# Router of a mixture-of-experts layer in three stages with the mean square taken on rows, and a one-hot product on another engine

## What is computed

```
h      = hidden_states                                  # 4096 tokens x 128
hf     = h * rsqrt(mean(h * h) + 1e-6) * rms_weight
logits = hf @ gate_w.T                                  # 8 experts
e      = exp(logits - max(logits))
top 2 of e, divided by their sum                        # weights and experts
out    = sum over the two of weight * (silu(hf @ w1.T) * (hf @ w3.T)) @ w2.T
```

## Time and profile before

| | us |
|---|---|
| median of 3 runs | 1366.04 |
| lowest, highest | 1364.01, 1376.72 |
| profiled execution, its own time | 1369.83 |
| profiled execution, its span | 1368.0 |
| router, slots and the hand-overs between, 966.96 to 1083.1 | 116.1 |

### The profile page before, as it was taken

One profiled execution on the slowest core, in us unless ns is written; L12 is line 12 of the kernel. 1 busy time (PEld: TensorE's weight loads), 2 busy tenths in 40 slices (PEclk: granted clock), 3 DMA queues, 4 the chain that ended last, 5 costly groups with the idle time before them and its releaser, 6 DMA issues. The chain is left out here.

```text
span 1368.0 us, 23917 instructions
## 1 busy us (share of the span) xinstructions
PE 1073.3 (78%) x6664; PEld 818.5 (60%) x6665; DVE 870.2 (64%) x1675; ACT 693.1 (51%) x1535; POOL 637.9 (47%) x938
## 2 busy tenths in 40 slices
PE   1999966899787799889998889973463399999950
PEld 1577742344386588778888788862242267777640
DVE  2477647201187599999999999992466633433327
ACT  1455432343244688888888888860242233433320
POOL 2000002100021689999999999980000556666630
PEclk9898857999999799999999999995555599999985
DMA  6000000111100200000000000003210011111135
GB/s 194 1 1 1 1 1 0 34 43 33 44 0 22 64 13 13 12 12 12 23 12 12 12 12 16 19 1 129 71 31 23 6 35 43 42 42 42 41 75 167
DMA packets 48617, 46.23 MB, mean 34 GB/s; under 512 B 4857, under 2 KB 44482, under 8 KB 48210
## 3 DMA queue, kind: packets, MB, share of 16 engines
q1 hardware_dynamic: 39474, 28.71, 7.3%
q0 software_dynamic: 4608, 9.45, 2.5%
q10 hardware_dynamic: 4496, 7.60, 1.6%
HBM read 36.74 MB, written 9.01 MB: 33 GB/s over the span
## 5 line engine op out<-in xcount | busy, mean ns | idle before, releaser
L1220 DVE TENSOR_TENSOR_SCAN s_hs<-s_dA,bank 128x1024 f32<-128x1024 f32 x128 | 291.5, 2277 | 11.2 <-PE bank L1617 10.5
L1477 POOL TENSOR_SCALAR s_dbuT<-s_dtuT,s_BT 128x256 f32<-128x256 f32 x512 | 242.3, 503 | 11.3 <-POOL s_bc L1415 5.4
L1338 ACT ACTIVATE s_dA<-s_dt,aneg 128x255 f32<-128x255 f32 x512 | 211.8, 495 | 0.2
L1617 PE MATMUL bank<-const,s_dbuT 128*128 128x128 f32 x1024 | 136.3, 277 | 3.1 <-POOL s_dbuT L1477 3.1
L1231 DVE TENSOR_TENSOR s_hc<-s_hs,bank 128x1024 f32<-128x1024 f32 (+1 forms) x128 | 130.2, 1017 | 5.0 <-PE bank L1644 1.6
L2142 PE MATMUL bank<-w,x_xT 128*128 x288 | 127.2, 565 | 5.4 <-issue 3.9
L1635 PE MATMUL bank<-const,s_hc 128*128 128x128 f32 x832 | 114.3, 276 | 21.1 <-DVE s_hc L1231 21.1
L1617 PEld LDWEIGHTS bank<-const,s_dbuT 128*128 128x128 f32 x1024 | 116.8, 143 | 6.5 <-POOL s_dbuT L1477 4.0
L1635 PEld LDWEIGHTS bank<-const,s_hc 128*128 128x128 f32 x832 | 95.7, 142 | 24.9 <-DVE s_hc L1231 24.9
L2180 ACT ACTIVATE x_a<-bank 128x448 f32<-128x448 f32 x72 | 39.2, 545 | 140.2 <-PE bank L2142 140.2
L2102 POOL DMA_INDIRECT x_xg<-hf_rows,x_src x72 | 69.8, 969 | 72.3 <-DVE x_src L2200 42.4
(11 more groups left out here) (303 smaller groups left out, 2332.1 us busy)
## 6 DMA issues: line engine op xcount, KB each, us to landing
s_Crow<-C_rows SPq DMA_DIRECT2D x48, 128.0 KB, 2.9
w<-in_w SPq DMA_DIRECT2D x16, 256.0 KB, 3.0
o_yr<-y_rows SPq DMA_DIRECT2D x8, 512.0 KB, 3.9
w<-in_w ACTq DMA_DIRECT2D x1, 3584.0 KB, 13.2
x_res<-in_x SPq DMA_DIRECT2D x4, 512.0 KB
gate<-gates_d SPq DMA_DIRECT2D x2, 1024.0 KB, 5.8
s_gate<-gates_d SPq DMA_DIRECT2D x2, 1024.0 KB, 7.4
hf_rows<-r_rows SPq DMA_DIRECT2D x8, 256.0 KB, 2.2
```

Source lines behind the costliest of these rows:

```text
L1220: dve.tensor_tensor_scan(flat(hs[:, j % 2]), flat(dA[:, j % RING]), bDbu[j % 2], 0.0, ALU.mult, ALU.add).then_inc(S["scanned"], 1)
L1338: ins = act.activation(dA[:, j % RING, h, n, 1:], dt[:, k, h, 1:], ACT.Exp, scale=m.aneg[:, h, 2 * j + n:2 * j + n + 1])
L1477: ins = pool.tensor_scalar(dbuT[:, j % RING, c, n, :], dtuT[:, k, c, :], BT[:, k, c, 2 * j + n:2 * j + n + 1], 1.0, ALU.mult, ALU.mult)
L1617: mm = pe.transpose(out[:, h, n, c * P:(c + 1) * P], dbuT[:, j % RING, c, n, h * P:(h + 1) * P], ident)
```

## The change

In the router three pairs are in flight (n0, n1, n2). Each engine's work is cut into small steps, and the bodies put them in a new order on each queue. The normalisation goes from VectorE to ScalarE, with a shift made by VectorE, as in the attention phase. The squares become the stationary side of four products with eight columns of ones, so that the mean square of a token stands on the token's partition: logarithm and exponential then take 4 columns. The logits are made from hT with a router matrix that is multiplied once with the norm's weight (`gw`), and scaled afterwards by the token's factor, 32 columns. The rows that go to memory are hT turned back, times the factor, so hf and its turning fall away; they lack the norm's weight, which is instead multiplied into `w13`, in place, by one instruction of GpSimd at the start of the slots phase. GpSimd makes the addition to x_res. PSUM banks, the factor and the stored rows get two buffers. In the slots phase the product with the tile numbers goes to VectorE, behind hot_lo, with the tile numbers in bf16. The core of the diff (the small steps of VectorE for which only the name of the semaphore is new are left out):

```diff
         def rounds(eng, body):
 
-            body(0, 0, None, None)
-            with eng.Fori(0, PAIRS // 2 - 1, 1) as r:
-                body(2 * r + 1, 1, 2 * r, 0)
-                body(2 * r + 2, 0, 2 * r + 1, 1)
-            body(PAIRS - 1, 1, PAIRS - 2, 0)
+            body(0, None, None, 0)
+            body(1, 0, None, 1)
+            with eng.Fori(0, (PAIRS - 2) // 2, 1) as r:
+                for k in range(2):
+                    body(2 * r + 2 + k, 2 * r + 1 + k, 2 * r + k, k)
+            body(None, PAIRS - 1, PAIRS - 2, 0)
             body(None, None, PAIRS - 1, 1)
...
+            def scaled_logits(n, w):
+                dve.wait_ge(S["lg_ps"], n + 1)
+                dve.wait_ge(S["rms"], n + 1)
+                dve.tensor_tensor(lgs[:], quarters(bL[w], E1), rrms[:, w].unsqueeze(2).broadcast_to([P, Q, E1]), ALU.mult)\
+                    .then_inc(S["lgs"], 1)
...
+            def expert_rows(n, w):
+                dve.wait_ge(S["rows_free"], n + 1)
+                dve.tensor_tensor(rows[:, w], quarters(bH[w], D), rrms[:, w].unsqueeze(2).broadcast_to([P, Q, D]), ALU.mult)\
+                    .then_inc(S["rows"], 1)
...
+            def body(n0, n1, n2, odd):
+                if n2 is not None:
+                    scaled_logits(n2, odd)
+                    greatest(n2)
+                    gated(n2, odd)
+                if n0 is not None:
+                    statistics(n0)
+                    moments(n0)
+                if n2 is not None:
+                    below_greatest(n2)
+                if n0 is not None:
+                    shifts(n0)
+                if n2 is not None:
+                    two_best(n2)
+                    share(n2)
+                    inverse(n2)
+                    places(n2)
+                    weights(n2)
+                    expert_rows(n2, odd)
+                    experts(n2)
+
+            for _ in range(2):
...
+            def inverse_rms(n, w):
+                act.wait_ge(S["ms_ps"], n + 1)
+                act.wait_ge(S["rows"], n + 1)
+                act.activation(lrms[:], quarters(bM[w], E1)[:, :, 0], ACT.Ln, bias=m.eps[:, 1:2])\
+                   .then_inc(S["lrms"], 1)
+                act.wait_ge(S["lrms"], n + 1)
+                act.activation(rrms[:, w], lrms[:], ACT.Exp, scale=-0.5).then_inc(S["rms"], 1)
+
+            def normalise(n):
+                act.wait_ge(S["shift"], n + 1)
+                if later(n):
+                    act.wait_ge(S["xT"], n)
+                for q in range(Q):
+                    act.activation(xn[:, q, :], m.x_res[:, n * Q + q, :], ACT.Identity, bias=shift[:, q:q + 1],
+                                   scale=rstd[:, q:q + 1]).then_inc(S["xn"], 1)
+
+            def modulate(n):
+                act.wait_ge(S["xT"], n + 1)
+                for k in range(2):
+                    act.activation(hT[:, k, :], bT[:, k * L:(k + 1) * L], ACT.Identity,
+                                   bias=m.modT[:, 1, 2, bass.ds(2 * n + k, 1)],
+                                   scale=m.modT[:, 1, 3, bass.ds(2 * n + k, 1)]).then_inc(S["h"], 1)
+
...
+            def body(n0, n1, n2, odd):
+                if n1 is not None:
+                    normalise(n1)
+                if n2 is not None:
+                    inverse_rms(n2, odd)
+                if n1 is not None:
+                    modulate(n1)
+                    squares(n1)
+                if n2 is not None:
+                    exponentials(n2)
+                if n0 is not None:
+                    layer_rstd(n0)
 
...
-            sp.sem_inc(S["rows_free"], 1)
-            with sp.Fori(0, PAIRS, 1) as r:
-                sp.wait_ge(S["rows"], r + 1)
-                sp.dma_start(m.hf_rows[bass.ds(r * Q * P, Q * P), :].rearrange("(q p) d -> p q d", p=P),
-                             rows[:]).then_inc(S["stored"], 16)
-                sp.wait_ge(S["stored"], 16 * (r + 1))
+            for _ in range(2):
                 sp.sem_inc(S["rows_free"], 1)
+            with sp.Fori(0, PAIRS // 2, 1) as r:
+                for k in range(2):
+                    n = 2 * r + k
+                    sp.wait_ge(S["rows"], n + 3)
+                    sp.dma_start(m.hf_rows[bass.ds(n * Q * P, Q * P), :].rearrange("(q p) d -> p q d", p=P),
+                                 rows[:, k]).then_inc(S["stored"], 16)
+                    sp.wait_ge(S["stored"], 16 * (n + 1))
+                    sp.sem_inc(S["rows_free"], 1)
+
+        @block.gpsimd
+        def _(pool):
+            def body(n0, n1, n2, odd):
+                if n2 is not None:
+                    pool.wait_ge(S["gh"], 2 * n2 + 4)
+                    xs = m.x_res[:, bass.ds(n2 * Q, Q), :]
+                    pool.tensor_tensor(xs, xs, gh[:], ALU.add).then_inc(S["added"], 1)
+
+            for _ in range(2):
+                pool.sem_inc(S["gh"], 1)
+            pool.sem_inc(S["added"], 1)
+            rounds(pool, body)
+            pool.wait_ge(S["added"], PAIRS + 1)
 
         @block.tensor
...
+            def turn(n):
+                pe.wait_ge(S["xn"], Q * n + Q)
+                if later(n):
+                    pe.wait_ge(S["h"], 2 * n)
+                for q in range(Q):
+                    mm = pe.transpose(bT[:, q * P:(q + 1) * P], xn[:, q, :], ident)
+                mm.then_inc(S["xT"], 1)
+
+            def mean_squares(n, w):
+                pe.wait_ge(S["sq"], n + 1)
+                for q in range(Q):
+                    mm = pe.matmul(bM[w][:, q * E1:(q + 1) * E1], sq[:, q * P:(q + 1) * P], m.ones128[:, 0:E1],
+                                   start=True, stop=True)
+                mm.then_inc(S["ms_ps"], 1)
+
+            def turn_back(n, w):
+                for q in range(Q):
+                    mm = pe.transpose(bH[w][:, q * D:(q + 1) * D], hf[:, q * P:(q + 1) * P], ident)
+                mm.then_inc(S["back_ps"], 1)
+
+            def logits(n, w):
+                pe.wait_ge(S["h"], 2 * n + 2)
+                pe.wait_ge(S["rows"], n + 1)
+                for q in range(Q):
+                    mm = pe.matmul(bL[w][:, q * E1:(q + 1) * E1], hf[:, q * P:(q + 1) * P], gw[:], start=True, stop=True)
+                mm.then_inc(S["lg_ps"], 1)
+
+            def body(n0, n1, n2, odd):
+                if n1 is not None:
+                    turn(n1)
+                    logits(n1, 1 - odd)
+                    mean_squares(n1, 1 - odd)
...
         @block.gpsimd
         def _(pool):
-            for c in range(SETS):
-                pool.wait_ge(s_same, c + 1)
-                if c >= 2:
-                    pool.wait_ge(s_used, c - 1)
-                tile = C_T72 + SET * c % TILES
-                pool.tensor_tensor(hot_hi[:, c % 2, 1], same_hi[:, c % 2],
-                                   m.const[:, tile:tile + SET].unsqueeze(2).broadcast_to([P, SET, MOE_TILES]),
-                                   ALU.mult).then_inc(s_tile, 1)
-
+            w13 = m.w13[:].rearrange("p e i -> p (e i)")
+            pool.tensor_scalar(w13, w13, m.gate1[:, E1:E1 + 1], 1.0, ALU.mult, ALU.mult).then_inc(s_w13, 1)
+            pool.wait_ge(s_w13, 1)
...
             lo_f, hi_f = (a[:].rearrange("p k t -> p (k t)") for a in (lo, hi))
+            tick(dve.tensor_copy(tiles[:], m.const[:, C_T72:C_T72 + TILES]))
+            settle()
             for c in range(SETS):
                 part = lambda a, n: a[:, SET * c:SET * (c + 1)].unsqueeze(2).broadcast_to([P, SET, n])
                 if c >= 2:
                     dve.wait_ge(s_row, c - 1)
                     dve.wait_ge(s_tile, c - 1)
+                    dve.wait_ge(s_used, c - 1)
                 dve.tensor_tensor(same_hi[:, c % 2], part(hi_f, MOE_TILES),
                                   m.const[:, C_T72:C_T72 + MOE_TILES].unsqueeze(1).broadcast_to([P, SET, MOE_TILES]),
                                   ALU.is_equal).then_inc(s_same, 1)
-                if c >= 2:
-                    dve.wait_ge(s_used, c - 1)
                 dve.tensor_tensor(hot_lo[:, c % 2], part(lo_f, P),
                                   m.const[:, C_I128:C_I128 + P].unsqueeze(1).broadcast_to([P, SET, P]),
                                   ALU.is_equal).then_inc(s_lo, 1)
+                tile = SET * c % TILES
+                dve.wait_ge(s_same, c + 1)
+                dve.tensor_tensor(hot_hi[:, c % 2, 1], same_hi[:, c % 2],
+                                  tiles[:, tile:tile + SET].unsqueeze(2).broadcast_to([P, SET, MOE_TILES]),
+                                  ALU.mult).then_inc(s_tile, 1)
 
             dve.wait_ge(s_used, SETS)
             pad = m.const[:, C_PAD:C_PAD + MOE_TILES]
```

207 lines of the change are left out of this document (90 added, 117 removed).

## The result

| | before | after | difference |
|---|---|---|---|
| median of the comparison, us (20 runs each) | 1369.78 | 1357.24 | ratio 0.9908, 95% interval 0.9887 to 0.9928 |
| span of the profiled execution, us | 1368.0 | 1360.0 | -8.0 |
| first statistics of the router to first work of slots, us | 78.87 | 65.08 | -13.8 |
| first work of slots to first work of the experts, us | 38.25 | 42.08 | +3.8 |

The kernel is 0.9% faster, 12.6 us, with an interval from 9.9 to 15.5; the ratio leaves out two slow runs of after, 1375.16 and 2222.81 us. The two stages of the profiled executions give -10.0. The rest of the span's difference lies outside: the router began 4.3 us later (971.25 for 966.96) and the part behind slots took 281.6 instead of 283.9.

The account below looks back on a forecast made before the run. No engine but a chain was taken to bound the router, and VectorE, then its wait for GpSimd, the slots. -17 + 6.2 - 2.0 = -12.8 us from 1366.04 gave 1353.2; own range 1350 to 1357, wide range 1345 to 1361.

Parts of the forecast that it names:

- The router: From first statistics to slots: shorter chain and work spread over three rounds save 17 us of 78.87.
- The rounds at full clock: Router: denser TensorE and single rounds at full level, so 17 us saved is taken instead of 16.3.
- TensorE's loop: Router round at the lower clock: turn, modulation, logits, mean squares and turning back sum to 6.5 us.
- The drain: Router's end, from the last shift to the last pair's rows, covered by nothing: 12.4 us.
- VectorE's 6.2: Router round: VectorE's own work and waits sum to 6.2 us, the round's length at full clock.
- The pass: Start of slots: GpSimd's scaling of w13 holds VectorE off the shared port, 6.2 us added.
- The product: Slots loop: one-hot product on VectorE makes a set 2.49 us in place of 2.76, 2.0 us less.
- No block: Rival, start of slots: GpSimd's pass does not stall VectorE, 2.4 to 6.2 us more saved; chance 0.12.
- Full clock: Rival, router: TensorE runs at full clock through denser rounds, gain 20.6 us, 1349.6 us; chance 0.18.
- A longer chain: Rival, router: steps fail to interlock, rounds 7.5 to 8 us, router gains only 8 to 10; chance 0.16.
- Slower, by the pass: Rival, slots: w13 scaling at 3.5 ns a column takes 25 us, kernel slower at 1372 us; chance 0.03.
- A middle rate: Rival, slots: w13 scaling at 1.2 ns a column takes 8.6 us, stall 8.4, kernel 1355.4 us; chance 0.11.

Follow-up runs that it names:

- Neither filler: Changed kernel, w13 scaled on ScalarE: four extra turnings per pair (0.9874); three extra 512-column products per pair, with squares in bf16, later weight loads, reordered steps (0.9742).
- The bf16 squares: Changed kernel with w13 scaled on ScalarE, plus the router's squares and ones columns in bf16: router 57.36 us, ratio 0.9824.

## Why the prediction was right or wrong

**The sum.** Predicted -12.8 us, measured -12.6 (9.9 to 15.5). The sign of each of the three parts is right, and the size of two; by the profiled executions they are -13.8, +5.96 and -2.1 where they stood at -17, +6.2 and -2.0. The router gave 3.2 us less than taken. The parts as measured add up to -10.0, so that the whole comes out within 0.2 us of the prediction is luck. In absolute terms 1353.2 was predicted and 1357.24 measured, just outside the forecast's own 1350 to 1357 and inside the wide range; 3.7 of these 4.0 us are before itself, whose median is 1369.78 over 20 runs and was 1366.04 over the three that the prediction started from.

**The router, -17 predicted, -13.8 measured.** The 3.2 us are 0.7 for a clock that did not come, 1.4 for the rounds and 1.1 for the drain; the rest cancels. Two of the signs that the prediction gave for being right did not appear: shifts are 6.77 us apart, not 6.3 to 6.6, and slots begin 65.1 us after the first statistics, not 61 to 63.

*The rounds at full clock.* The working at the lower level gave -16.3. On top the prediction added 0.7, because TensorE would be denser and single rounds at the full level were in the trace of before. They vanished: 0.50 granted after, for 0.59. TensorE did become denser, by about as much as taken: in the rounds it is busy for 79% of the time (31.63 of 40 us from 980) where it was for 70% (41.85 of 60 us from 975). The step that failed is the one from denser to faster, for which the prediction had only the mean of 0.59. Why the clock stays down is open. Neither filler brought the full level for more than part of the rounds.

*TensorE's loop, 6.5 predicted, 6.77 measured.* The terms as written add up to 6.56, so 0.21 was missing. The mis-sized terms are the logits and the mean squares. Both were priced at 1.57, from start to start of the next group; they take 1.73 and 1.70. The hand-over from modulation to logits took 0.13 for 0.05, the turning back 0.89 for 0.99, the turn 1.06 for 1.11. The 0.24 before the modulation and its 1.02 stand as predicted. The weight loads (PEld) suggest the reason. In before the first load of the logits starts at 1005.42, 0.21 ahead of the first product:

```profile
1005.42 1.83 PEld L1862 LDWEIGHTS bank<-gate,r_hf 128*128 128x128 f32 x8
```

In after it starts with the product, at 1004.53, since it loads the hT that TensorE has just waited for. Counted from first load to first load of the next group (the turning back's is at 1007.75), the logits take 1.57 in before, and logits and mean squares 1.66 and 1.56 in after. So the price of a group was about right, and what it left out is one load of 0.2 us that nothing hides. This is a reading of the rows; no run tests it.

Over the phase: first shift after 2.0 us (2.2 predicted), second 5.25 later (5.4), third 6.82 (6.6), the five others 33.87 together (32.5), from the last shift to the last rows 13.53 (12.4), hand-over to slots 3.61 (3.45).

*The drain, 12.4 predicted, 13.53 measured.* The failed term is the first, 1.8 from the last shift to the turn:

```profile
1019.39 1.65 ACT L1867 ACTIVATE r_xn<-x_res,r_shift,r_rstd 128x128 f32<-128x128 f32 x4 [0.23 <-DVE r_shift L1758]
...
1022.40 1.06 PE L1945 MATMUL bank<-const,r_xn 128*128 128x128 f32 x4
```

The shift is at 1019.19, the four normalised tiles are ready at 1021.04, and the turn starts at 1022.40, 3.2 us after the shift. Until then TensorE has the logits, mean squares and turning back of the pair before in its queue, so it is 1.4 us that the prediction's drain, which follows the last pair alone, did not have. The other steps together took some 0.3 less than their price.

*Which loop is the bound:* TensorE, as predicted. The bf16 squares show it, for they touch nothing else. VectorE's 6.2, the second bound of the prediction, was too large: it holds a round of 5.84. And the loop that stands next to TensorE's was not among those summed. The prediction added each engine's queue by itself and found ScalarE at 4.5; the ring through three engines, 5.84, is longer than ScalarE's queue. No run undoes a part of the router's rewrite, so how much of the 13.8 us comes from the third pair in flight, from the narrow mean squares, or from the turning that fell away is not shown.

**The pass, +6.2 predicted, 5.96 measured.** Its rate was taken as 0.86 ns a column from the difference of two forms of the earlier trace rows and is 0.87 (6.24 us for 7168). The upper bound for that rate, 3.5 ns, was not GpSimd's slowest: its product in the earlier trace rows takes 2.07 us for 576 columns, 3.6 ns. The stall is as the earlier trace rows show it for 0.61 us. Only the place differs: the hot pair came first, and the block fell on the next product of two tensors, m_before. The Trainium skill ("SBUF — State Buffer", Who interferes with whom) says the pair of ports is held for a whole instruction and the other side fully blocks. By that rule, the trace agrees for 6.24 us, and on GpSimd's side for 0.53, by which its pass is longer where it meets the hot products.

**The product, -2.0 predicted, -2.1 and -1.8 measured.** 2.48 a set for 2.49. The full price was right: 0.75 for 576 columns, the same as same_hi with a float32 input, though its two inputs and its output are bf16. The Trainium skill ("VectorE: DVE Perf Modes", What auto-detection actually checks) asks step 1 of every tensor for the doubled rate. By that rule, the trace agrees: the tile number is one element read 72 times.

**The rivals.** *No block:* fell for after; that VectorE's first products come first happened, but the pass did not fit the wait that follows. Started after the counts it is a saving of 2.4, the near end of what the rival gave. *Full clock:* fell; the clock went the other way. *A longer chain:* 6.77 is between the 6.5 taken and the 7.5 from which it was told; the steps interlock in the rounds, and TensorE's queue explains the whole of 6.77, while the ring is there, 0.9 below. In the drain the turn did stand behind TensorE's own tail, as this rival has it. *Slower, by the pass:* fell, 0.87 ns a column is far from the 2.65 at which it turns the sign. *A middle rate:* fell by the same number.

## What to carry to other kernels

Before work is given to GpSimd because it is idle, look at what VectorE does in that time: beside products of two SBUF tensors a long GpSimd instruction costs up to its whole length (5.96 us of 6.77 here, 3.56 of 6.24 when it began in a wait of VectorE), and the same pass on an idle ScalarE cost nothing. To find a pipelined loop's bound, add up each engine's queue and also the rings that close over several engines through the order of their queues. Price a group of short products from load to load, and add the first load where its stationary side is what the engine waits for. In the drain, follow the last item behind what its engines still owe the one before. And read the wait at the stage's edge first: ordering one load behind another was worth more here (some 15 us by the stages) than the whole rewrite (10).

## What the runs showed of the hardware

- GpSimd's hold on VectorE is per instruction. Sixteen queued pieces cost VectorE 2.37 us where one pass cost 5.96, and fifteen of them spread over 11.32 us. A copy that reads a PSUM bank was not held (m_tot, 0.43); an instruction that reads one SBUF tensor, of 8 columns, was (m_full, 0.43 for 0.17).
- GpSimd scales 7168 columns in place in 6.24 us, ScalarE in 6.27.
- A float32 product of eight moving columns with a 128 by 128 stationary side costs 0.43 us at the lower clock level (1.70 to 1.73 for four, each in two passes), and the loads of the stationary side are busy for nearly all of it (PEld 1.83 of 1.85). In bf16 four take 0.25.
- A load of 1 MB that took 21.6 us beside the loads of the expert weights takes 5.7 without them.
- The granted clock of the router was 0.50 in after, with TensorE busy for 79% of the rounds. With four more turnings a round it was 0.50 but for 3.4 us at 1.00; with three more products of 512 columns, in another order, 0.76 for 20 us and then 0.50. At 1.00 a group of four float32 products of eight columns took 0.9 us from start to start where it took 1.7 at 0.50.
- ScalarE's table load took 1.28 us in its queue, and cost the router 0.66 where it came behind the wait for the gate rows.
